# A two-layer convolution kernel: one more slot for the row pairs, one more pair of products split by columns, and TensorE's program written out without its loop

## What is computed

```python
x = x + _L0_conv_ref(_gn(x), ...)   # 3x3 depthwise, then three 64x64 channel mixes
x = x + _L1_conv_ref(_gn(x), w)     # sign(x), 3x3 full conv with sign(w) * mean|w|
```

## Time and profile before

| | |
|---|---|
| Time, median of 3 runs | 1913.36 us (1906.17 to 1913.38) |
| The profiled execution: its own time, its span | 1914.54 us, 1912.4 us |
| PE busy | 1797.5 us (94%), 35562 matmuls |
| PEld busy | 1502.8 us (79%) |
| DVE busy | 1595.4 us (83%) |
| ACT busy | 1303.5 us (68%) |
| POOL busy | 534.9 us (28%) |
| Granted TensorE clock over the span | 0.998 |
| DMA: moved, mean | 271.50 MB, 142 GB/s |

### The profile page before, as it was taken

How to read it: one execution, slowest core, us unless ns; L and a number is a source line. 1 busy time by engine, 2 the same in 40 slices (tenths; PEclk the granted TensorE clock), 3 DMA queues, 4 the chain that set the end, 5 groups by cost and what they waited for, 6 DMA issues and landing times.

```text
span 1912.4 us, 81089 instructions
## 1 busy us (share of the span) xinstructions
PE 1797.5 (94%) x35562; PEld 1502.8 (79%) x35562; DVE 1595.4 (83%) x2578; ACT 1303.5 (68%) x1367; POOL 534.9 (28%) x285
## 2 busy tenths in 40 slices
PE   0099999999999999999999999999999999999997
PEld 0087777999987776999988887899988677687775
DVE  5678889888898889988898888988888888877776
ACT  2066776777777776777767777777767777677774
POOL 0032332333332222333223332233322333233331
PEclk9999999999999999999999999999999999999999
DMA  9934655555555555555655555555655555432223
GB/s 205 219 76 139 159 149 145 158 152 151 151 145 156 154 154 142 147 160 150 152 144 153 151 151 153 141 163 152 153 144 147 152 150 150 105 85 75 73 74 99
DMA packets 279270, 271.50 MB, mean 142 GB/s; under 512 B 16576, under 2 KB 278848, under 8 KB 279104
## 3 DMA queue, kind: packets, MB, share of 16 engines
q1 hardware_dynamic: 279104, 269.23, 55.3%
HBM read 134.95 MB, written 134.22 MB: 141 GB/s over the span
## 4 chain that ended last, share of the span: by engine, by line
PE 89%; DVE 4%; SPq 4%; issue 1%; ACT 1%; DMA 1%; DVEq 0%; ACTq 0%
PE psA L484 77%; PE psB L484 12%; SPq L249 3%; DMA ring<-in_x 1%; ACT xh L365 1%; DVE bnt L685 1%; DVE ring L885 0%; DVE ring L851 0%; DVE aggr L792 0%; DVE psL L881 0%; SPq L256 0%; DVE pk L862 0%; DVE xc L843 0%; ACT xn L361 0%; DVE ring L890 0%
## 5 line engine op out<-in xcount | busy, mean ns | idle before, releaser
L484 PE MATMUL psA<-xh,W 64*64 64x512 f16 (+1 forms) x19456 | 1668.1, 360 | 15.5 <-ACT xh L365 9.4
L484 PEld LDWEIGHTS psA<-xh,W 64*64 64x64 f16 x19456 | 1152.9, 106 | 186.1 <-issue 21.4
L484 PE MATMUL psA<-xl,W 64*64 64x512 f16 (+1 forms) x9984 | 1142.7, 359 | 1.0 <-issue 1.0
L301 POOL TENSOR_TENSOR xl<-xc,xn 128x1024 f16<-128x1024 f32 (+2 forms) x264 | 532.0, 2017 | 1295.7 <-ACT xn L361 1295.7
L484 PEld LDWEIGHTS psA<-xl,W 64*64 64x64 f16 x9984 | 624.5, 106 | 89.1 <-issue 4.3
L484 PE MATMUL psB<-pk,W 64*64 64x512 f16 (+3 forms) x5568 | 638.8, 341 | 2.9 <-DVE pk L862 2.4
L365 ACT ACTIVATE xh<-xc 64x1024 f16<-64x1024 f32 (+1 forms) x528 | 543.3, 1032 | 9.4
L851 DVE SCALAR_TENSOR_TENSOR ring<-psA,columns,ring 128x1024 f32<-128x1024 f32 x256 | 328.4, 1283 | 211.4 <-PE psA L484 211.3
L361 ACT ACTIVATE xn<-xc 128x1024 f16<-128x1024 f32 (+2 forms) x264 | 272.0, 1033 | 302.0 <-PE psA L484 234.7
L685 DVE BATCH_NORM_STATS2 bnt<-ring 128x6 f32<-128x512 f32 x512 | 326.8, 681 | 40.8 <-DMA ring<-in_x 40.7
L484 PEld LDWEIGHTS psB<-pk,W 64*64 64x64 f16 x5568 | 337.4, 106 | 29.8 <-issue 6.4
(11 more groups left out here) (90 smaller groups left out, 125.4 us busy)
## 6 DMA issues: line engine op xcount, KB each, us to landing
out_y<-ring SPq DMA_DIRECT2D x512, 256.0 KB, 3.3
ring<-in_x SPq DMA_DIRECT2D x448, 256.0 KB, 3.9
ring<-in_x SPq DMA_DIRECT2D x32, 512.0 KB, 13.9
pk<-in_w1T SPq DMA_DIRECT2D x2, 144.0 KB, 7.7
ring<-in_w1n SPq DMA_DIRECT2D x2, 144.0 KB, 7.6
grp<-in_same_group SPq DMA_DIRECT2D x1, 64.0 KB, 6.0
ring<-in_dw SPq DMA_DIRECT2D x2, 2.2 KB, 5.4
ring<-in_att SPq DMA_DIRECT2D x1, 16.0 KB, 2.0
```

The costliest lines, as they stand in the source:

```text
L301: ins = nc.gpsimd.tensor_tensor(xl[:, slot:slot + rows, 1:W + 1], xc[:, j:j + rows], xn[:, k:k + rows, 1:W + 1], ALU.subtract)
L484: mm = pe.matmul(bank[out0:out0 + C, c0:c1], weights[src0:src0 + C, :], src[src0:src0 + C, slot:slot + rows, width[0]:width[0] + width[1]] ...
```

## The change

The slot buffers `xh` and `xl` get a seventeenth slot and new numbers: chunk q keeps its row pairs at 4q + 1 to 4q + 4, and the last row pair of each q = 3 chunk (but an image's last) is written a second time, to slot 0, by ACT (`together`) and POOL (`again`). An image's first chunk becomes one copy of five row pairs on ACT. `pk` keeps 16 slots with the numbering modulo 16, so DVE packs a q = 3 chunk in two pieces. In `step_one` the neighbour pair of high by high products for dx = 1 (g = 1) is split by columns: its first 256 columns move to the crossing stream (k = 13), its last 256 stay in the straight one (k = 24). Each stream then has 31 full pairs and one of half width. Everything after k = 13 in the crossing stream moves back by one place; the wait for `cross_left` stays in front of straight pair 15 and is now raised by crossing pair 13, `sign_left` stays in front of straight pair 21 and is now raised by crossing pair 19, `straight_left` is waited for in front of crossing pair 20. PE's loop goes away.

```diff
-SLOTS = 16
+SLOTS = 17
@@
     def kept(ch):
         if ch.at(0):
-            return [(SLOTS - 1, 0, 1), (0, 1, G)]
-        return [(G * ch.q, 1, G - 1 if ch.at(NC - 1) else G)]
+            return [(0, 0, 1), (1, 1, G)]
+        return [(G * ch.q + 1, 1, G - 1 if ch.at(NC - 1) else G)]
+
+    def again(ch):
+        return [(0, G, 1)] if ch.q == 3 and not ch.at(NC - 1) else []
+
+    def packed(ch):
+        return [(G * ch.q + 1, 1, G - 1)] + again(ch) if ch.q == 3 else kept(ch)
+
+    def together(ch):
+        return [(0, 0, G + 1)] if ch.at(0) else kept(ch) + again(ch)
@@
-        pk = sb("pk", [128, SLOTS, HPW], F16)
+        pk = sb("pk", [128, SLOTS - 1, HPW], F16)
@@ low_part, on POOL
-                for slot, j, rows in kept(ch):
+                for slot, j, rows in kept(ch) + again(ch):
@@ high_part, the copies to xh, on ACT
-                    for slot, j, rows in kept(ch):
+                    for slot, j, rows in together(ch):
@@ pack, on DVE
-                for slot, j, rows in kept(ch):
+                for slot, j, rows in packed(ch):
@@ PE
             def columns(ch, first, pairs, width):
-                slot = (G * ch.q + first - 1) % SLOTS
-                cut = min(pairs, SLOTS - slot)
-                out = [(slot, cut, 0, cut * width)]
-                if cut < pairs:
-                    out.append((0, pairs - cut, cut * width, pairs * width))
+                slot = G * ch.q + first
+                return [(slot if slot >= 0 else SLOTS - 2, pairs, 0, pairs * width)]
+
+            def sign_columns(ch, first):
+                slot = (G * ch.q + first) % (SLOTS - 1)
+                cut = min(G, SLOTS - 1 - slot)
+                out = [(slot, cut, 0, cut * HW)]
+                if cut < G:
+                    out.append((0, G - cut, cut * HW, G * HW))
                 return out
@@
+            def beside_plain_first(ch, dx):
+                k = G * ch.par
+                return pair(True, psA[:, ch.par, 2 * W:3 * W], xn, dx, W, (W0[:, 0, dx, 1, :], [(k, 1, 0, W)]),
+                            (W0[:, 0, dx, 0, :], [(k + 2, 1, 0, W)]), False, False)
+
+            def beside_second(ch, dx):
+                bank = psA[:, ch.par, 3 * W:4 * W]
+                wt = W0[:, 0, dx]
+                mm = piece(0, 0, bank, wt[:, 3, :], xh, columns(ch, 2, 1, W), (dx, W), False, False)
+                if not ch.at(NC - 1):
+                    mm = piece(C, C, bank, wt[:, 2, :], xh, columns(ch, 4, 1, W), (dx, W), False, False)
+                return mm
@@ straight_layer0
+                elif split and g == 1 and i == 7:
+                    mm = beside_second(a, 1)
@@ crossing_layer0
+                moved = 2 if split else 1
@@
+                elif g == 1 and i == 13:
+                    mm = beside_plain_first(a, 1)
@@ step_one
                 for k in range(32):
-                    if k < 13:
-                        crossing_layer0(img, a, k, 1)
-                    elif k < 19:
-                        crossing_signs(img1, u, k - 13)
-                    elif k < 31:
-                        crossing_layer0(img, a, k - 6, 1)
+                    if k < 14:
+                        crossing_layer0(img, a, k, True)
+                    elif k < 20:
+                        crossing_signs(img1, u, k - 14)
+                    else:
+                        crossing_layer0(img, a, k - 6, True)
@@ image
-                with pe.Fori(first, NC // 4 - 1) as v:
-                    for q in range(4):
-                        step_one(img, Chunk(v, q), img, Chunk(v, q - LAG))
+                for i in range(4 * first, NC - 4):
+                    step(img, i)
```

More of the change, by code:

```diff
@@ L467, in above_of @@
                 if ch.at(0) and g == 0:
-                    return [(SLOTS - 1, 1, W, 2 * W)]
+                    return [(0, 1, W, 2 * W)]
                 return columns(ch, 2 * g - 1, 2, W)
@@ L512, in sign_own @@
             def sign_own(ch, dx, cross, start, stop=False):
-                at = columns(ch, 0, G, HW)
+                at = sign_columns(ch, 0)
                 return pair(cross, psB[:, ch.par], pk, dx, HW, (W1[:, dx, 0, :], at), (W1[:, dx, 1, :], at),
@@ L517, in sign_beside @@
             def sign_beside(ch, dx):
-                above = columns(ch, -1, G, HW)
+                above = sign_columns(ch, -1)
                 if ch.at(0):
-                    above = [(SLOTS - 1, 1, HW, 2 * HW), (0, 2, 2 * HW, G * HW)]
-                below = columns(ch, 1, G, HW)
+                    above = [(0, G - 1, HW, G * HW)]
+                below = sign_columns(ch, 1)
                 if ch.at(NC - 1):
@@ L537, in beside_plain, with straight_layer0 @@
                             (W0[:, 0, dx, 0, :], [below]), False, False)
-            def straight_layer0(img, a, j, moved):
+            def beside_plain_first(ch, dx):
[9 more added lines that the diff above has]
+                return mm
+            def straight_layer0(img, a, j, split=False):
                 n = img * NC + a.i
@@ L547, in straight_layer0 @@
                     bank_free(cross_left, n + 1)
-                i += moved if g == 1 and i >= 6 else 0
+                i += 1 if g == 1 and i >= 6 else 0
                 last = g == 1 and i == 14
@@ L559, in straight_layer0, with crossing_layer0 @@
                     mm.then_inc(a_mm, 1)
-            def crossing_layer0(img, a, j, moved):
+            def crossing_layer0(img, a, j, split=False):
                 n = img * NC + a.i
+                moved = 2 if split else 1
                 g, i = (1, j) if j < 12 + moved else (0, j - 12 - moved)
@@ L614, in step_alone @@
                     if k < 13:
-                        crossing_layer0(img, a, k, 1)
+                        crossing_layer0(img, a, k)
                     elif k >= 17:
-                        crossing_layer0(img, a, k - 4, 1)
-                    straight_layer0(img, a, k, 1)
+                        crossing_layer0(img, a, k - 4)
+                    straight_layer0(img, a, k)
                     if between is not None and k == 10:
@@ L624, in step_one @@
                 for k in range(32):
-                    if k < 13:
-                        crossing_layer0(img, a, k, 1)
-                    elif k < 19:
-                        crossing_signs(img1, u, k - 13)
-                    elif k < 31:
-                        crossing_layer0(img, a, k - 6, 1)
+                    if k < 14:
[4 more added lines that the diff above has]
+                        crossing_layer0(img, a, k - 6, True)
                     if k < 21:
-                        straight_layer0(img, a, k, 1)
+                        straight_layer0(img, a, k, True)
                     elif k < 24:
@@ L635, in step_one @@
                     else:
-                        straight_layer0(img, a, k - 3, 1)
+                        straight_layer0(img, a, k - 3, True)
                     if between is not None and k == 10:
```

## The result

The change made the kernel slower: 1949.57 us median of 4 runs (1945.48 to 1953.66) against 1913.37 of 4 runs beside it, ratio 1.0185, 95% interval 1.0165 to 1.0205. The forecast was 1895, its range 1881 to 1921, so the time lies 29 us above the range. First the page: busy time, the queues, the chain by engine and by line, and two groups.

The account below looks back on a forecast made before the run. PE was taken to bound the kernel, carrying 89% of the chain of waits. From the profiled 1914.5 us, -27.3 - 1.5 + 2.7 + 8 gave 1896.4; that execution lay 1.2 above the median, so 1895, range 1881 to 1921.

Parts of the forecast that it names:

- Part 1: PE's steady step: straight stream goes from 32 pairs to 31 and a half-width one, 0.108 us a step, -27.3 us.
- Rival N: PE's products start in program order, so the halves don't meet and the split saves nothing: 1920 us, chance 0.07.
- Part 2: PE's waits for `cross_left` and `sign_left`, before straight pairs 15 and 21, come closer without delaying the chunk: cost 0.
- Rival W: Straight pairs 15 and 21 come late at their waits in every step, 0.10 us each: 1946 us, chance 0.11.
- Parts 1 to 5: All terms but the loop's removal: -27.3, 0, -1.5, 0 (second copies on ACT and POOL) and +2.7 us.
- part 3: Matmul cuts at the slot buffers' wrap go: -1.5 us, between 0 and -2.5.
- part 5: Change of image, bounded by DVE: PE's saving lost over four steps, `pack` dearer, ACT cheaper: +2.7 us.
- Part 6: PE's loop goes, so 156 more steps run on fetched code: +8 us, between 0 and 25.
- Rival H: Fetching PE's written-out code is dear, 20 to 30 us: 1907 to 1917 us, chance 0.13.
- theory G: From the experiments: PE's sequencer stops at an increment carrying a wait and loses its lead, so late code is felt.

Follow-up runs that it names:

- the two kernels without stalls: Increments of an unused semaphore taken out of the changed kernel (1878.7 us) and of the kernel before with its loop written out (1905.2 us).

## Why the prediction was wrong, point by point

- **Part 1, right.** A quiet step is 6.83 us, and the half-width pair is there, from PE's timeline of the changed kernel:

```profile
718.47 0.46 PE L499 MATMUL psA<-xn,W 64*64 64x512 f16 x2
...
718.69 0.35 PE L499 MATMUL psA<-xn,W 64*64 64x256 f16 x2
```

Rival N is out with the step's length, and with it the order of starts that "TensorE: Matmul & The Clock Gate" of the Trainium skill gives, where the two quarters are concerned.
- **Part 2, right.** No step is 7.0 us by the closer waits. The first load behind `cross_left` comes at 719.15, 0.17 us after the recorded end of straight pair 12 (718.98; forecast 0.13), and straight pair 15 is on the beat of 0.22 us:

```profile
719.04 0.38 PE L499 MATMUL psA<-xl,W 64*64 64x512 f16 x2
...
719.25 0.38 PE L499 MATMUL psA<-xh,W 64*64 64x512 f16 x2
```

Rival W, the only one that was to end slower, is out; the kernel did end slower, by another path.
- **Parts 1 to 5 together** can be read from the two kernels without stalls: 1878.7 against 1905.2 is -26.5 us; the parts gave -27.3 - 1.5 + 2.7 = -26.1. The loop back (1885.8 against 1911.6) gives -25.8. The terms come out one by one too, by the median distance of two starts of the clock line: 6.937 us before, 6.928 with the slots and 6.821 with the split as well, over 255 steps -2.3 (part 3, forecast -1.5, at most -2.5) and -27.3 (part 1); what the 255 steps take over their quiet length is 7.5 us in the kernel before without stalls and 9.8 in the changed one with the order of waits and increments turned round, +2.3 for part 5's +2.7. Matmuls fell by 2430, not some 2900: the split itself adds two a step, which I had left out (with the slots alone they are 32634, 2928 fewer).
- **Part 6 is the step that failed**: +8 us with an upper end of 25. By the same pairs the stalls cost the changed kernel 1949.6 - 1878.7 = 70.9 us and the kernel before 1913.4 - 1905.2 = 8.2, so the price was +62.7; putting only the loop back gives 63.8. Rival H had the sign and went to 30 at most. I read the price per step off seven images' chunks 1 to 7 and took stalls for chance, spread evenly. They go with the block's place in the step, and they need the waits that the sequencer carries. A loop's program samples few places, 12 written steps an image here; the written-out program drifts through them all and stays in the bad ones for 8 steps. Above all I did not ask why a sequencer that reads ahead should ever be short: the 0.61 us at 1032.42 was the hint, and the instruction that carries the wait stood in the code.
- On the rule of the Trainium skill, "Runtime: NRT & Kernel Launch", "Instruction fetch mechanics": in the changed kernel the trace went against it (126.9 us of "issue" before one group of loads); with the waits on loads it agrees (1.0 us), so what I weighed as one rule against one row were two states of one thing. The same section gives PE room for 2048 instructions, and the trace is in line with it: a body of about 1064 is kept (no packet from 413 to 513 us), one of about 2128 is not (296 packets). It also says that a taken branch to code outside a window of two pages, of 256 instructions each, has to fetch first. That a body of 4.2 pages is kept goes against two pages, and the measurement decides; that a branch to code that isn't there stalls agrees (0.21 against 4.8 us by the median). The Trainium skill, "Perfetto Trace Analysis", "Sequencer-only Instruction (DRAIN, etc)", draws what theory G says: such an instruction waits in the sequencer, which reads the next only after it. The last runs agree: 1949.6 us by the one carrier, 1877.3 by the other.

**Open.** Why a packet comes late in one place and in time in another. In the changed kernel a packet's transfer starts up to 6.4 us after the first load of the block before, with the order turned round at most 2.8; a lead of 1.2 us does not cover that difference. Traffic is a part of it (no stores, 52 us less), but which transfers a packet stood behind was not separated, nor why the kernel of seventeen slots ran quiet at places where others stood. A kernel with the loop and the waits on loads was not run.

## What to carry to other kernels

Where an engine's code is fetched as it runs, put a wait on an instruction of the engine's queue rather than on one that the sequencer executes itself; here that order alone was worth 72 us of 1950. Before a loop is written out or an edit is judged, look at "issue" as releaser before the weight loads and at the code's DMA queue: if fetches are felt, an edit's own effect and that of its code length mix, and an A/B of the edit alone misleads (2 us seen of a 27 us gain, 6 us of one that should be nearly nothing). A loop body that is not kept can cost more than no loop: here 4.2 blocks were kept and 8.3 were not.

## What the runs showed that I had not expected

128 instructions that do nothing, ahead of the first step, moved each group of slow steps by some 10 to 14 steps and left their number nearly as it was. A loop body of 8.3 blocks costs 4 to 10 us at each jump back, part of it because TensorE's granted clock is down to half for some 8 us after the stop, and makes the kernel 149 us slower than one of 4.2. And the order of two instructions, a wait and an increment that nobody needs, decides whether a third of the code's packets come just in time or all of them some microseconds early.
